# New planner costs and priorities, the last softmax unit on VectorE, and other filler turns in a one-core macaron block

## What is computed

```python
x = x + 0.5 * ffn(layernorm(x))
x = x + attn(layernorm(x))      # softmax over the keys, 8 heads of 32
x = x + 0.5 * ffn(layernorm(x))

def ffn(x):
    h = rmsnorm(x, gamma1)
    q = h @ Wq + bq                              # 16 heads of 16
    k, v = split((h @ Wdown + bdown) @ Wup + bup)
    att = softmax(einsum('bthd,btgd->bthg', q, k) / 4)   # each token: heads against heads
    x = x + einsum('bthg,btgd->bthd', att, v) @ Wo + bo
    h2 = rmsnorm(x, gamma2)
    gate = softmax(h2 @ Wg + bg)                 # 8 experts, all used
    return x + einsum('btd,edf,bte->btf', h2, We, gate)
```

## Time and profile before

| what | value |
|---|---|
| median of 3 runs | 996.87 us (995.22 to 998.73) |
| profiled execution, its own time | 998.04 us |
| its span, first to last instruction | 996.1 us |
| PE busy | 956.9 us (96%) |
| DVE busy | 857.5 us (86%) |
| ACT busy | 640.0 us (64%) |
| POOL busy | 787.9 us (79%) |
| mean granted TensorE clock | 0.997 |

### The profile page before, as it was taken

One profiled execution on the slowest core, in us unless ns is written; L12 is line 12 of the kernel. 1 busy time (PEld: TensorE's weight loads), 2 busy tenths in 40 slices (PEclk: granted clock), 3 DMA queues, 4 the chain that ended last, 5 costly groups with the idle time before them and its releaser, 6 DMA issues.

```text
span 996.1 us, 28140 instructions
## 1 busy us (share of the span) xinstructions
PE 956.9 (96%) x11065; PEld 757.0 (76%) x11065; DVE 857.5 (86%) x1387; ACT 640.0 (64%) x1287; POOL 787.9 (79%) x866
## 2 busy tenths in 40 slices
PE   8799999999999989999999999887999999999998
PEld 7678878888888866666666666556788888887886
DVE  7899889888887379999999999997998988888863
ACT  5667467466576367777777877776665764755752
POOL 6888797896875548999899899988767977958744
PEclk9999999999999999999999999999999999999999
DMA  7021000000000000000000000000000000000001
GB/s 226 2 76 44 2 2 3 1 2 1 3 1 2 1 1 3 1 2 2 2 1 3 1 2 2 2 2 2 2 2 23 23 2 23 23 2 23 2 23 43
DMA packets 8399, 14.47 MB, mean 15 GB/s; under 512 B 1993, under 2 KB 5964, under 8 KB 8270
## 3 DMA queue, kind: packets, MB, share of 16 engines
q1 hardware_dynamic: 8270, 12.67, 3.7%
HBM read 8.48 MB, written 4.19 MB: 13 GB/s over the span
## 4 chain that ended last, share of the span: by engine, by line
PE 82%; DVE 9%; POOL 4%; issue 4%; ACT 1%; DVEq 0%; POOLq 0%; ACTq 0%
PE psum L511 53%; PE psum L920 6%; PE psum L930 6%; PE psum L946 5%; PE psum L697 3%; PE psum L687 3%; DVE late L1284 3%; DVE oT L1278 2%; PE psum L829 1%; PE psum L771 1%; PE psum L844 1%; PE psum L881 1%; POOL kvx L1690 1%; DVE qc L1116 1%; DVE kvcs L1168 0%
## 5 line engine op out<-in xcount | busy, mean ns | idle before, releaser
L511 PE MATMUL psum<-we,h 128*128 128x512 f32 x1536 | 387.1, 399 | 2.8 <-DVE X L1252 1.9
L511 PEld LDWEIGHTS psum<-we,h 128*128 128x128 f32 x1536 | 279.6, 188 | 63.3 <-issue 3.3
L1278 DVE TENSOR_REDUCE oT<-psum 128x128 fp32r<-128x1024 f32 x128 | 155.0, 1218 | 12.9 <-PE psum L920 12.6
L1252 DVE SCALAR_TENSOR_TENSOR X<-psum,gate,X 128x256 f32<-128x256 f32 x260 | 123.8, 477 | 45.7 <-PE psum L511 34.1
L1481 ACT ACTIVATE kvx<-psum 128x1024 f32<-128x1024 f32 x126 | 128.9, 1024 | 53.2 <-PE psum L930 42.7
L1418 ACT ACTIVATE late<-psum,gate 128x256 f32<-128x256 f32 x252 | 104.6, 467 | 81.2 <-PE psum L511 48.1
L1690 POOL TENSOR_TENSOR late<-kvx,late 128x2048 f32<-128x2048 f32 x31 | 121.3, 3913 | 34.7 <-ACT late L1488 23.9
L1284 DVE TENSOR_REDUCE late<-kvx 128x256 f32<-128x2048 f32 x63 | 143.4, 2276 | 0.0
L1690 POOL TENSOR_TENSOR kvx<-kvx,late 128x2048 f32<-128x2048 f32 x32 | 124.9, 3903 | 1.6 <-ACT late L1488 0.8
L1641 POOL TENSOR_TENSOR late<-late 128x512 f32<-128x512 f32 x63 | 82.0, 1301 | 49.7 <-ACT late L1418 49.5
L1366 ACT ACTIVATE kvx<-kvcs,mask 128x512 f32<-128x512 f32 x132 | 88.9, 735 | 22.7 <-DVE kvcs L1140 13.2
(11 more groups left out here) (184 smaller groups left out, 1935.0 us busy)
## 6 DMA issues: line engine op xcount, KB each, us to landing
X<-in_L_attn_hidden_states SPq DMA_DIRECT2D x7, 512.0 KB, 5.9
out<-X SPq DMA_DIRECT2D x7, 512.0 KB, 2.6
X<-in_L_ffn_We SPq DMA_DIRECT2D x2, 1024.0 KB, 10.4
X<-in_L_attn_hidden_states SPq DMA_DIRECT2D x2, 256.0 KB, 3.2
out<-X SPq DMA_DIRECT2D x1, 384.0 KB, 2.3
late<-in_L_ffn_turned SPq DMA_DIRECT2D x1, 257.0 KB, 4.3
kvx<-in_L_ffn_Wq SPq DMA_DIRECT2D x1, 256.0 KB, 2.9
kvx<-in_L_ffn_Wup SPq DMA_DIRECT2D x2, 128.0 KB, 2.6
```

The costliest lines, as they stand in the source:

```text
L511: ins = e.matmul(out_ap, l, r, start=(n == 0), stop=(n == len(terms) - 1))
L1252: e.scalar_tensor_tensor(out=xi, in0=psum[:, u % 3, w * D:(w + 1) * D], scalar=gate[k % 2][:, i, 2 * n + w:2 * n + w + 1], in1=xi, op0=ALU ...
L1278: e.tensor_reduce(mr[g // 2 % 2][:, queries(g)], heads(g), AX.X, ALU.max).then_inc(a_max, 1)
```

## The change

- In `all_steps`, the planned costs of columns, spread, gate_last, gate_out and of hT, down and q of job 0 are raised.
- normalise of the last unit (63) gets the engine DVE, a cost of 2250 and its own predecessors; the instruction is the same (`weigh`), with a semaphore of its own, a_norm_last, on which values(63) and out_turn(16) wait.
- SOONER, FIRST and SAME get other values.
- The turns are 14 at the beginning, then 24 ahead of attend(0), 4 ahead of attend(1), 8 ahead of values(63), 4 ahead of attend(16), 8 ahead of oT(8,0), 8 ahead of scores(17): 70 in all. The wait on a_exp stands ahead of the turns of values(63) and for the last count.

```diff
-    put("PE", 200, ("columns", 0), ("rows", 0))
+    put("PE", 950, ("columns", 0), ("rows", 0))
...
-    put("PE", 750, ("spread", 0), ("last", 0))
-    put("PE", 1400, ("spread", 1), ("last", 0))
+    put("PE", 1300, ("spread", 0), ("last", 0))
+    put("PE", 2750, ("spread", 1), ("last", 0))
...
-    put("PE", 280, ("gate_last", 0), ("gate_fold", 0))
+    put("PE", 470, ("gate_last", 0), ("gate_fold", 0))
...
-    put("PE", 1350, ("gate_out", 0), ("gate_row", 0), ("turned", 0))
+    put("PE", 2550, ("gate_out", 0), ("gate_row", 0), ("turned", 0))
...
-            put("PE", 435, ("hT", s, p), ("xs", s, p), ("down", s - 1, before), ("q", s - 1, p))
+            put("PE", 435 if s else 870, ("hT", s, p), ("xs", s, p), ("down", s - 1, before), ("q", s - 1, p))
...
-            put("PE", size(940, 490), ("down", s, w), ...
+            put("PE", size(940, 490) if s else 1040, ("down", s, w), ...
...
-            put("PE", 1460, ("q", s, p), ("hT_lo", s, p), ("scores", c - 2), ("split_lo", 1))
+            put("PE", 1460 if s else 2100, ("q", s, p), ("hT_lo", s, p), ("scores", c - 2), ("split_lo", 1))
...
+    steps["normalise", units - 1] = ("DVE", 2250, (("inverse", units - 1), ("values", units - 3), ("a_total", units - 1)))
     return steps
...
-          "down": -2692, "expert": -3003, "ct": -4707, "q_up": -7504, "gate_wo": -13718, "h2_lo": -14792, "rows": -15769,
...
-          "val_A": -60744, "a_stats": -62679, "a_rstd": -68230, "xs2": -68582, "x1_base": -77317, "gate_out": -77453,
...
+SOONER = {"gate_log": 341195, "spread": 311980, "mask": 297620, "scores": 270266, "at_zero": 224213, "oT": 222772,
+          "a_hT": 217051, "gate_row": 211125, "gate_out": 205316, "a_exp": 203873, "rms2": 189078, "a_hT_lo": 172422,
...
+          "v_bias": 6038, "q": 5329, "xs": 3256, "values": 2974, "norm": 1976, "down": 1427, "key": 134, "h2T": -2267,
...
-SAME = 9767
+SAME = 11607
...
+        idle = {("attend", 0): 24, ("attend", 1): 4, ("values", units - 1): 8,
+                ("scores", 2 * B + 1): 8, ("attend", 2 * B): 4, ("oT", B, 0): 8}
+
         def pe_program(e):
             e.wait_ge(s_const, 1)
-            turn_nothing(e, 16)
+            turn_nothing(e, 14)
...
-                if piece == ("scores", 0):
-
-                    turn_nothing(e, 16)
-                elif piece == ("key", 0, 1):
-                    turn_nothing(e, 10)
-                elif piece == ("shift", halves - 17):
-
-                    turn_nothing(e, 9, 7)
-                elif piece == ("q", B, 1):
-
-                    e.wait_ge(a_exp, halves - 1)
-                    turn_nothing(e, 12)
-                elif piece == ("values", units - 1):
-                    turn_nothing(e, 8)
-                elif piece in (("oT", B, 0), ("attend", 2 * B + 1)):
-                    turn_nothing(e, 6)
+                if piece in idle:
+                    if piece == ("values", units - 1):
+                        e.wait_ge(a_exp, halves)
+                    turn_nothing(e, idle[piece])
...
-                    e.wait_ge(a_norm, u + 1)
+                    e.wait_ge(*((a_norm, u + 1) if u < units - 1 else (a_norm_last, 1)))
...
+        def weigh(e, u):
+
+            e.wait_ge(a_inv, u + 1)
+            if u >= 2:
+                e.wait_ge(a_values, u - 1)
+            return e.tensor_tensor(prob[u % 2][:, :, :].rearrange("p g n -> p n g"), exponentials(u)[:, :, :],
+                                   rec[u % 2][:, :].unsqueeze(2).to_broadcast([P, NQ, G]), ALU.mult)
...
+                elif name == "normalise":
+                    weigh(e, piece[1]).then_inc(a_norm_last, 1)
...
-                        e.wait_ge(a_norm, units)
+                        e.wait_ge(a_norm_last, 1)
...
-                    e.wait_ge(a_inv, u + 1)
-                    if u >= 2:
-                        e.wait_ge(a_values, u - 1)
-                    e.tensor_tensor(prob[u % 2][:, :, :].rearrange("p g n -> p n g"), exponentials(u)[:, :, :],
-                                    rec[u % 2][:, :].unsqueeze(2).to_broadcast([P, NQ, G]),
-                                    ALU.mult).then_inc(a_norm, 1)
+                    weigh(e, u).then_inc(a_norm, 1)
```

31 lines of the change are left out of this document (16 added, 15 removed).

## The result

The change makes the kernel slower. Its median is 1003.58 us (1002.66 to 1004.44, 6 runs) beside 998.84 us for the kernel before on the same chip; the ratio is 1.0054, with a 95% interval of 1.0039 to 1.0069, or 5.4 us. The forecast was 993.0 us; the result lies on the other side of no change and above the range. The profiled execution took 1003.67 us, its span is 1001.6 us. Two executions of the study at some 1310 us, one of the kernel before and one of change_30, both with a mean granted clock of 0.652, are left out of all ratios.

The account below looks back on a forecast made before the run. PE was taken to bound the long stages, with only the start and the change-over having time to give. The six terms sum to -3.9 us: 994.1 for the profiled execution, 993.0 us for the median; range 987.5 to 1001.0.

Parts of the forecast that it names:

- Term 1: At the beginning, 14 turns instead of 16 let PE's next work start sooner: -0.4 us.
- Term 2: In the first sequence, new planned costs move gate_out ahead of the first down: -0.6 us, bounds -1.4 and +1.8.
- Term 3: Around the first attends, turns are removed and 24 and 4 placed ahead of attend(0) and attend(1): -1.0 us.
- What is removed, 3.0 us, brings nothing: At the start, turns taken out ahead of key(0,1) and scores(0) change nothing, since DVE and POOL set the pace.
- +1.4 if the clock falls in spite of them: At the first attends, the slow end: the clock drops although 24 turns stand ahead of attend(0), +1.4 us.
- Term 4: In the change-over, the last unit's product on DVE takes 2.4 us and brings values(63) sooner: -1.1 us.
- The bound of +1.9: In the change-over, attend(16) comes up to 1.9 us late if DVE's product lands whole ahead of pair 16's work.
- What is late next is at(16): In the change-over, once the product is on DVE, DVE's at(16), which attend(16) needs, is the next late step.
- Term 5: In the change-over, 28 turns from values(63) to scores(17) fill waits and may hold the clock: -0.8 us.
- Term 6: New priorities elsewhere, mainly the two long stages: taken as 0, with 7.35 us of idle PE time to win or lose.
- The slower rival: Expert products wait for their three banks as DVE does other work first: +8.0 us, sum 1001.0, chance 0.20.
- the first rival: At start and change-over, turns hold no clock and DVE's product gains nothing: -1.4 us, 995.5, chance 0.25.

Follow-up runs that it names:

- change_30: The kernel before with 38 instead of 8 turns ahead of values(63); 994.37 us, ratio 0.9968.
- start_turns: The kernel before with only the start's turns changed (14 at the beginning, 24 ahead of attend(0), 4 ahead of attend(1)); 1000.69 us, ratio 1.0037.
- gate_early: The kernel before with gate_out ahead of the first down and gate_wo behind split_lo 3; 997.62 us, ratio 1.0001.
- after: The changed kernel itself, with the whole change, against the kernel before; 1003.58 us, ratio 1.0054.
- new_turns: The kernel before with all the new turns, at the start and in the change-over, and nothing else changed; 1000.10 us, ratio 1.0025.
- after_more: The changed kernel with the turns of before plus 10 each ahead of val(0), attend(0) and hT(1,1); 1002.86 us, ratio 1.0045.
- old_turns: The changed kernel with the filler turns of the kernel before; 1001.72 us, ratio 1.0045.
- change_13: The kernel before with 21 instead of 8 turns ahead of values(63); 995.21 us, ratio 0.9976.
- dve_product: The kernel before with only the last unit's product moved to VectorE, behind key_turn(8,1); 1001.98 us, ratio 1.0041.
- late_new: The kernel before until mid-attention, then the changed priorities, the last unit's product on VectorE and the new change-over turns; 1002.58 us, ratio 1.0055.
- late_order: late_pool with the filler turns of the kernel before; 1000.80 us, ratio 1.0030.
- late_order2: late_order with the last unit's product one step later on GpSimd, behind q_zero(8,0); 1002.59 us, ratio 1.0051.
- late_pool: late_new with the last unit's product back on GpSimd, behind at_zero; 1004.80 us, ratio 1.0068.
- prod_alone: The kernel before with six extra products on VectorE at its end; dense ones take 2.29 us each, scattered ones 3.62 to 3.63 us.
- stage_order: The kernel before until 685 us of planner's time, then the changed priorities alone, product on GpSimd and old turns; 1002.92 us, ratio 1.0049.
- start_47: The kernel before with 47 more turns at the start and 12 fewer in front of the change-over; 994.40 us, ratio 0.9975.

## Why the prediction was wrong

**Term 1** (two turns fewer, -0.4): it cannot be seen by itself; start_turns holds it and is slower.

**Term 2** (costs, gate_out, -0.6): gate_out moved as forecast, to 12.97. The gain failed: 0.1 us, with an interval of about 1.2 us to either side, in gate_early. The slip of the first down (forecast up to 1.8 us, measured 1.66 us in gate_early, 2.74 us in after, where it also begins later) and what the move saves cancel to within the interval; the runs don't separate them. A size, not a sign.

**Term 3** (turns at the start, -1.0): the step that failed is "What is removed, 3.0 us, brings nothing". The 26 turns taken out were what PE did between short waits from 19 to 28 us. Without them the clock was low from 20.7 to 34.3 us (new_turns), or low for 3.4 us from 30.0 on, behind a wait of 3.02 us (start_turns). The times of the executions bear this out in part. The nine of new_turns with a mean granted clock of 0.988 to 0.991 take 999.10 to 1001.62 us; the two with 0.993 and 0.997 take 997.45 and 997.76, close to the 997.27 of the kernel before on that chip. Of start_turns the three with 0.995 or more take 998.12 to 1000.39 us, above 997.46 even so; the overrun of the wait is left there. Between kernels the mean clock is a weak witness, since it leaves out the low stretch ahead of the first rise: 0.990 for new_turns and 0.9905 for start_turns, against 0.993 and 0.996 for the kernel before on the same chips (medians of all executions). The end marked "+1.4 if the clock falls in spite of them" was the right mechanism and too small, +2.5 to +3.7 us in the old order. In the changed order the same turns weigh less: after_more and old_turns, with more turns and with the old ones, both have 1.0045, and after has 1.0054. Nor was the whole price offered for the clock, 1.74 us, there to be had. change_30 has the very instructions of the kernel before until 676 us, and its low clock lies elsewhere:

```profile
core 0: us, PE busy (x) PEld busy (x) DVE busy (x) ACT busy (x) POOL busy (x), PEclk, DMA share, GB/s
37.00:41.00 4.00, 3.80 (x70) 3.47 (x59) 3.90 (x9) 0.35 (x1) 4.00 (x4) 1.00 0.02 4
...
68.00:70.00 2.00, 2.00 (x6) 1.54 (x6) 1.70 (x6) 0.71 (x2) 0.01 (x1) 0.50 0.04 8
...
686.00:688.00 2.00, 2.00 (x72) 1.75 (x66) 1.29 (x2) 0.94 (x2) 2.00 (x4) 1.00 0.03 8
...
```

The clock is 1.00 at 37 to 41 us, where the earlier trace rows had 0.50, and 0.50 at 68. Its first expert product comes 1.44 us sooner than before, and at the 97th both are within 0.04 us. Ten of the traces (before, change_13, change_30, dve_product, late_new, late_order, late_order2, late_pool, prod_alone and stage_order) have the same start. Behind 30 us the clock is low between 32 and 41 us in four of them, between 67 and 72 in five, and not at all before 600 us in one, late_order. The 97th expert matmul starts at 92.87 to 93.95 us in eight of the nine with a low stretch, and at 92.29 in late_order. By this comparison the fall in the kernel before (93.07) cost some 0.8 us by then, not 1.74. (late_pool has a second long low stretch, from 8.6 to 25.7 us, and starts it at 95.48.) One profiled execution showed one of the places where the clock may fall, and the forecast took it for the kernel's.

**Term 4** (the product, -1.1): forecast 2.4 us for the product, measured 3.71 us alone and 4.80 us beside POOL. The row was right in engine and in having two SBUF operands, but was another operation, and its output was dense. The bound of +1.9 was exceeded: +4.1 us in the old order, where attend(16) slipped by 3.3 us. "What is late next is at(16)" held. Even on the forecast's terms the gain for attend(16) was smaller than its 0.5 us: it began at 681.38, not 681.6, so 0.34 us were open to it. In the changed order DVE did at least the statistics first. What its place costs there is not shown: late_new is 1.3 us faster than late_pool, within the intervals, and late_pool has a fault of its own; late_order2, with the product on GpSimd and the old turns, has 1.0051 where late_new has 1.0055.

**Term 5** (change-over turns, -0.8): in the profiled execution the clock was 0.58 at 683 to 687 us, so they held nothing there. Their wait on the last exponentials cost nothing: the 8 turns begin right behind scores(16), at 680.61. The runs don't price them alone: old_turns against after says 0.9 us for all turns, new_turns against start_turns says that in the old order they gained rather than lost, 1.2 us; both are within the intervals.

**Term 6** (priorities elsewhere, 0): this is the step that weighs most. Terms 3 and 4 were off by about as much in the old order, but this is the one that reaches the whole loss with the old turns and the product on GpSimd. "That is the most to be won, and no reason excludes as much lost" was in the text, and the sum took 0. The new order loses 3 to 5 us by itself (late_order, late_order2; stage_order with the priorities alone). The loss has two shapes in the traces: at the change-over (late_order2), where q(8,0) comes late and PE's steps of job 9 stand in front of those of job 8 and wait for POOL, and in the second stage (stage_order), where a DVE instruction that POOL blocks holds back the taking-out of expert products.

**The rivals.** The slower rival, with chance 0.20, was the side that came, and nearly the size (+4.1 on the median of 996.87, against +5.4). Its mechanism is shown in stage_order, once for 4.03 us and not in each of 16 jobs; in after itself it is 1.0 us, less than the 1.9 us of the kernel before. That its sum came so near is luck. Of the first rival, "DVE's product gains nothing" is shown, and the 4 us that were to speak for it came. "The turns hold no clock" isn't: taking them away cost 2.5 us or more, of which the overrun of 24 turns ahead of attend(0) explains 1.4, and the two executions of new_turns with the higher clock, few as they are, lost next to nothing. 47 more turns (start_47) don't speak for it either. Their mean clock is 0.991 in the median of 12 executions, but the profiled one has 0.991 because its clock rose early, at 4.2 us, and the fall from 7.7 to 17.9 us is counted, where the kernel before was as low with no record of it; from 18 to 60 us it has 1.00. The Trainium skill says in "TensorE: Matmul & The Clock Gate", part 4, that transposes don't count as busy as other matmuls do. The runs speak against that rule for this kernel: in after, after_more, late_order and start_47 the clock rose at 4.2 to 4.4 us, when PE had done nothing but its 14 or 16 first turns, which are transposes. It doesn't rise there each time; in the kernel before the same turns were followed by the lower level until 16.8 us, and what PE did ahead of the execution no trace shows.

Of the signs that the forecast named, gate_out came near its place (12.97 for 12.5), the clock was 1.00 at 38 us and low at 686, values(63) came at 683.90 and not before 679.5, and PE's idle time in the long stages was 3.81 and 5.92 us for 4.1 and 3.3.

The forecast's general error was to add the two places where the time had to give and leave the order's change at zero, when nearly every name's constant in SOONER had changed.

## What to carry over

When a planner's priorities all change, price the new order as a risk with a sign, from the waits that a single blocked instruction can cause, and not as zero. Before moving an operation to a "faster" engine, look for a row of the same layout of output and for what stands beside it on the engine that shares its access to SBUF. Try a few doses of filler in waits and measure each: some dozens of small instructions moved this kernel by 0.24 to 0.32% to the good where they were added and by 0.25 to 0.37% to the bad where they were moved, and one profiled execution told the reason of neither. Before comparing mean clocks, look where the first record of each trace begins.

## What the hardware showed that was not expected

- PE pauses of 0.6 to 2.0 us inside runs of tiny matmuls (64 in 1.1 us), all 48 of them, in 20 traces, in front of record 194 or 195 of a block of 256 records of PE's stream (matmuls, weight loads and semaphore waits). Filler transposes added anywhere ahead removed some and created others.
- The same product on VectorE takes 2.29 us with a dense output and 3.62 us with consecutive elements far apart.
- An instruction of 4 elements a partition on GpSimd took 3.48 us instead of 0.19 us beside a VectorE product of two SBUF operands, and a VectorE operation with a median of 1.22 us took 4.57 us behind two groups of GpSimd.
- The place of a stretch at half clock in the first 100 us varies between executions of the same instructions (32 to 41 us in four, 67 to 72 us in five, none behind 30 us in one), and so does the first rise of the clock (4.3 to 5.9 us in six of these ten, 16.5 to 17.8 us in four).
- The view's clock counts as full what lies ahead of the first record: 1.00 for the first 16.8 us of the kernel before, in which a turn took 0.23 us, twice its length at the full clock.
